# Recall's queries: from a stage of their own into the selection's prologue of the memory stage

## The reference, cut to what matters

```python
q = (x @ Wq).reshape(b, n, HEADS, DIM) * DIM ** (-0.5)     # x [4,1025,64], Wq [64, 8*64]
kv_scores, indices = _pk(x, Wq_pk, pk_keys)                # top 16 of 64x64 product keys, per head
...
k = jnp.einsum('bnhk,bnhkd->bnhd', kv_scores, keys_table[ind])
v = jnp.einsum('bnhk,bnhkd->bnhd', kv_scores, values_table[ind])
sim = jnp.einsum('bihd,bjhd->bhij', q, k)                  # causal softmax, then @ v, then @ Wo
```

## Time and profile before

| | |
|---|---|
| median of 3 runs | 5455.95 us (5443.48 to 5458.74) |
| profiled execution, its own time | 5452.82 us |
| its span | 5451.1 us, 70887 instructions |
| PE busy | 4506.6 us (83%) |
| DVE busy | 3522.2 us (65%) |
| ACT busy | 2183.1 us (40%) |
| POOL busy | 936.1 us (17%) |
| granted clock of TensorE, mean | 0.878 of full speed |

### The profile page before, as it was taken

How to read it: one execution, slowest core, us unless ns; L and a number is a source line. 1 busy time by engine, 2 the same in 40 slices (tenths; PEclk the granted TensorE clock), 3 DMA queues, 4 the chain that set the end, 5 groups by cost and what they waited for, 6 DMA issues and landing times. The chain is left out here.

```text
span 5451.1 us, 70887 instructions
## 1 busy us (share of the span) xinstructions
PE 4506.6 (83%) x24566; PEld 2736.8 (50%) x24566; DVE 3522.2 (65%) x8760; ACT 2183.1 (40%) x3699; POOL 936.1 (17%) x1106
## 2 busy tenths in 40 slices
PE   7793999999999999999998799899479999961004
PEld 3461444444444444444554455555379889861002
DVE  7547777777777777777552677776455555774325
ACT  1351444444444444444443445445333434320001
POOL 0123111111111111111000000000033320005771
PEclk8555999999999999999997899999589999985556
DMA  2003354666555556655543511110110010000110
GB/s 69 8 1 66 101 134 123 130 124 140 130 135 130 130 125 128 132 121 139 141 117 103 138 32 36 27 34 1 22 28 15 7 20 6 7 2 7 20 14 12
DMA packets 324643, 389.21 MB, mean 71 GB/s; under 512 B 119857, under 2 KB 274749, under 8 KB 323492
## 3 DMA queue, kind: packets, MB, share of 16 engines
q1 hardware_dynamic: 233848, 185.45, 16.8%
q0 software_dynamic: 58368, 172.46, 10.5%
q10 hardware_dynamic: 32076, 26.80, 2.7%
HBM read 313.90 MB, written 70.64 MB: 71 GB/s over the span
## 5 line engine op out<-in xcount | busy, mean ns | idle before, releaser
L1056 PE MATMUL mem_kv<-mem_weights,mem_table 128*128 128x456 f32 x4608 | 1955.5, 546 | 0.0
L1292 DVE SCALAR_TENSOR_TENSOR mem_weights<-mem_above,mem_exps 128x912 f32<-128x912 f32 x1152 | 1272.7, 1105 | 668.6 <-ACT mem_exps L1172 665.6
L1172 ACT ACTIVATE mem_exps<-mem_above 128x912 f32<-128x912 f32 x1152 | 1069.7, 929 | 913.7 <-PE mem_above L1043 913.5
L1056 PEld LDWEIGHTS mem_kv<-mem_weights,mem_table 128*128 128x128 f32 x4608 | 871.2, 189 | 567.1 <-issue 451.1
L1043 PE MATMUL mem_above<-mem_operands,mem_selector 123*128 123x456 bf16 x2304 | 636.5, 357 | 41.1 <-DVE mem_weights L1292 25.1
L2195 DVE TENSOR_REDUCE mha_chunk_max<-mha_max_scores 114x1 f32<-114x342 f32 x864 | 438.1, 512 | 327.5 <-PE mha_max_scores L2063 308.5
L2086 PE MATMUL mha_sums<-mha_probs,mha_value_wide 114*72 114x114 f32 (+1 forms) x5184 | 607.8, 261 | 14.2 <-ACT mha_probs L2177 14.2
L2086 PEld LDWEIGHTS mha_sums<-mha_probs,mha_value_wide 114*72 114x72 f32 (+1 forms) x5184 | 559.8, 143 | 23.4 <-issue 21.3
L1043 PEld LDWEIGHTS mem_above<-mem_operands,mem_selector 123*128 123x128 bf16 x2304 | 218.3, 98 | 558.3 <-issue 445.9
L2177 ACT ACTIVATE mha_probs<-mha_scores 114x912 f32<-114x912 f32 x324 | 297.6, 930 | 380.9 <-PE mha_scores L2075 358.0
L944 POOL DMA_DIRECT2D mem_table<-in_L_ffn_tables_dram x288 | 153.3, 538 | 1353.7 <-PE mem_kv L1056 1348.4
(11 more groups left out here) (588 smaller groups left out, 5237.0 us busy)
## 6 DMA issues: line engine op xcount, KB each, us to landing
mem_table<-in_L_ffn_tables_dram POOLq DMA_DIRECT2D x288, 512.0 KB
mem_operands<-scratch_second_scores SPq DMA_DIRECT2D x216, 256.5 KB
mem_operands<-scratch_first_scores SPq DMA_DIRECT2D x288, 128.2 KB
mem_inv_z<-scratch_inv_z SPq DMA_DIRECT2D x72, 228.0 KB
scratch_second_scores<-mem_sel_parts ACTq DMA_DIRECT2D x81, 171.0 KB
scratch_first_scores<-mem_sel_parts ACTq DMA_DIRECT2D x108, 114.0 KB
scratch_mem_keys<-mem_kvT SPq DMA_DIRECT2D x72, 114.0 KB, 9.2
scratch_mem_values<-mem_value SPq DMA_DIRECT2D x72, 114.0 KB
```

Of the source, the lines that this page charges most:

```text
L1056: last = nc.tensor.matmul(acc[k][:, 0:SPAN], table[:, k, ch, :], W[:, J % 3, c, :], start=(ch == 0), stop=(ch == CHUNKS - 1))
L1172: nc.scalar.activation(E[:, J % 2, :, :], psD[J % 2][:, :, 0:SPAN], ACT.Exp).then_inc(exped, 1)
L1292: nc.vector.scalar_tensor_tensor(W[:, J % 3, :, :], psD[J % 2][:, :, 0:SPAN], 0.0, E[:, J % 2, :, :], ALU.is_ge, ALU.mult).then_inc(weight ...
```

## The change

The query stage is removed from `recall_stage`. Its 16 rounds are put into `memory_stage`'s prologue, one in every 12 phases (`QEVERY = 6 * 32 / 16`): PE's products of round n ahead of its part of phase 12n, ACT's copies of it ahead of its part of phase 12n + 6, SP's stores of all 16 rounds ahead of `store_theta(0)`. The rounds borrow buffers that the loop over items needs only later: `Wq` lies in the loop's `kvT`, the staged queries (two buffers in place of four) in its `weights`, the products in the PSUM buffers of `above` (two of the three chunks) and `kv` (the third). So a copy is two activations, of 684 and 342 columns, in place of one of 1026. Two new waits stand at the end of the prologue, PE's for the last copies and DVE's for the last stores.

```diff
+        q_w, q_mm, q_cp = s.sem("query_weights_in"), s.sem("query_mm"), s.sem("query_copied")
+        q_st = [s.sem(f"query_stored{k}") for k in range(2)]
+        wq = kvT[0:DIM, :, :].rearrange("p k n -> p (k n)")[:, 0:PH * DIM]
+        qout = W[:, :, :, :].rearrange("p a c n -> p (a c n)")
+        QROUNDS = BATCH * PH // 2
+        QEVERY = AHEAD * PHASES // QROUNDS
...
+            sp.dma_start(wq, io["L0_ffn_Wq"]).then_inc(q_w, 16)
+
+            def store_queries(n):
+                b, hh = divmod(n, PH // 2)
+                sp.wait_ge(q_cp, n * 2 + 2)
+                sp.dma_start(qD[hh * 128:(hh + 1) * 128, b, :], qout[:, n % 2 * PAD:(n % 2 + 1) * PAD]).then_inc(q_st[n % 2], 16)
...
+            for n in range(QROUNDS):
+                store_queries(n)
             store_theta(0)
             settled(0)
             load(0)
...
+                sp.wait_ge(q_st[k], QROUNDS // 2 * 16)
...
+            def queries(n):
+                b, hh = divmod(n, PH // 2)
+                if n >= 2:
+                    pe.wait_ge(q_cp, n * 2 - 2)
+                for c in range(3):
+                    to = psD[n % 2][:, c, 0:HALF] if c < 2 else acc[n % 2][:, 0:HALF]
+                    last = nc.tensor.matmul(to, wq[:, hh * 128:(hh + 1) * 128], xT[0:DIM, b, c * HALF:(c + 1) * HALF],
+                                            start=True, stop=True)
+                last.then_inc(q_mm, 1)
+
+            pe.wait_ge(q_w, 16)
             for u in range(AHEAD):
                 for r in range(PHASES):
+                    n, at = divmod(u * PHASES + r, QEVERY)
+                    if at == 0:
+                        queries(n)
                     select(u, r)
+            pe.wait_ge(q_cp, QROUNDS * 2)
             pe.wait_ge(sel_done, SEL_DONE)
             above(0)
...
+            def copy_queries(n):
+                act.wait_ge(q_mm, n + 1)
+                if n >= 2:
+                    act.wait_ge(q_st[n % 2], n // 2 * 16)
+                to = qout[:, n % 2 * PAD:(n % 2 + 1) * PAD]
+                nc.scalar.activation(to[:, 0:2 * HALF].rearrange("p (c n) -> p c n", c=2), psD[n % 2][:, :, 0:HALF], ACT.Copy,
+                                     scale=DIM ** -0.5).then_inc(q_cp, 1)
+                nc.scalar.activation(to[:, 2 * HALF:PAD], acc[n % 2][:, 0:HALF], ACT.Copy, scale=DIM ** -0.5).then_inc(q_cp, 1)
+
             for u in range(AHEAD):
                 for r in range(PHASES):
+                    n, at = divmod(u * PHASES + r, QEVERY)
+                    if at == QEVERY // 2:
+                        copy_queries(n)
                     select(u, r)
...
+            dve.wait_ge(q_mm, QROUNDS)
+            for k in range(2):
+                dve.wait_ge(q_st[k], QROUNDS // 2 * 16)
...
-def recall_stage(nc, io, H, xT, ident, kTD, vD, edge):
-    qD = nc.dram_tensor("scratch_mem_q", [PH * DIM, BATCH, PAD], F32).ap()
-    with ExitStack() as ctx:
-        s = Space(nc, ctx, "memq")
...
-            for n in range(ROUNDS):
-                b, hh = divmod(n, PH // 2)
-                sp.wait_ge(cp, n + 1)
-                sp.dma_start(qD[hh * 128:(hh + 1) * 128, b, :], qo[:, n % 4, :]).then_inc(st[n % 4], 16)
...
+def recall_stage(nc, io, H, xT, ident, qD, kTD, vD, edge):
```

More of the change, by code:

```diff
@@ L793, with memory_stage @@
 OPS = 12
-def memory_stage(nc, io, xT, ident, aD, bD, tD, zD, kTD, vD):
+def memory_stage(nc, io, xT, ident, aD, bD, tD, zD, qD, kTD, vD):
     with ExitStack() as ctx:
@@ L1315 @@
 RECALL_MAX = 96
-def recall_stage(nc, io, H, xT, ident, kTD, vD, edge):
-    qD = nc.dram_tensor("scratch_mem_q", [PH * DIM, BATCH, PAD], F32).ap()
-    with ExitStack() as ctx:
-        s = Space(nc, ctx, "memq")
[L1328 to L1339, removed]
-            for n in range(ROUNDS):
-                b, hh = divmod(n, PH // 2)
-                sp.wait_ge(cp, n + 1)
-                sp.dma_start(qD[hh * 128:(hh + 1) * 128, b, :], qo[:, n % 4, :]).then_inc(st[n % 4], 16)
[L1344 to L1364, removed]
-                nc.scalar.activation(qo[:, n % 4, :].rearrange("p (c n) -> p c n", c=3), ps[n % 2][:, :, 0:HALF], ACT.Copy,
-                                     scale=DIM ** -0.5).then_inc(cp, 1)
+def recall_stage(nc, io, H, xT, ident, qD, kTD, vD, edge):
     with ExitStack() as ctx:
@@ L3037, in memory_layer @@
     norm_stage(nc, "norm_mem", H, xT, ident)
+    qD = nc.dram_tensor("scratch_mem_q", [PH * DIM, BATCH, PAD], F32).ap()
     kTD = nc.dram_tensor("scratch_mem_keys", [PH, DIM, NODES], F32).ap()
@@ L3043, in memory_layer @@
     zD = nc.dram_tensor("scratch_inv_z", [TILES, PH, SPAN], F32).ap()
-    memory_stage(nc, io, xT, ident, aD, bD, tD, zD, kTD, vD)
+    memory_stage(nc, io, xT, ident, aD, bD, tD, zD, qD, kTD, vD)
     edge.open(nc, ctx)
-    recall_stage(nc, io, H, xT, ident, kTD, vD, edge)
+    recall_stage(nc, io, H, xT, ident, qD, kTD, vD, edge)
 def heads_layer(nc, io, H, xT, ident, edge):
```

## The result

The changed kernel takes 5437.0 us (median of 12 runs) against 5455.4 (12 runs): a ratio of 0.9966, 95% interval 0.9957 to 0.9975, so 18.4 us less. I had said 42 to 44 less, and a range from 5397 to 5434. One of the 12 runs took 8043.6 us at a mean granted clock of 0.55; it is left out of the ratio. The profiled execution has a span of 5434.7 us, 16.4 under that of before.

What follows compares the result with a forecast made beforehand. PE bounds loop and query stage; the prologue ends by its unit chain and SP's `load(0)`. Removing 62.4 us and adding 20.4 gave -42.0: 5410.8 from the profile, 5414 by the median, said 5412; range 5397 to 5434.

Steps and rivals of the forecast that it cites:

- What went: Query stage between memory stage and attention: all 62.4 us go, while the 3.4 us between stages stay.
- What a round costs: Per round in the prologue: PE 3.4 us at clock 0.50, ACT's two copies 1.2 us, SP's issue 0.32 us.
- Unit by unit: Prologue units 0 to 4: rounds and copies that miss PE's idle delay the chain, so unit 5 starts 13.6 us later.
- SP's queue: Prologue's end: threshold stores wait behind store 15 and land last, so `load(0)` goes out at 556.5, 20.4 us late.
- starving: Rival, chance 0.17: query stores land late beside the part stores, copy 12 waits for store 10; 5429 to 5436 us.
- the other edits cost nothing here: Prologue: the `Wq` load, the new waits of PE and DVE at its end and extra semaphores add 0 us.
- the loop and the attention are unchanged, and read `qD` from DRAM as before: Stages after the prologue: no change in time; the loop's length was to stay 2378.6 us.
- Better hidden: Rival, chance 0.14: prologue at clock 1.00, a round 1.7 us, no unit slips; -55 to -57 us, 5398 us.
- Slower: Rival, chance 0.03: no round hides, each adding 3.4 + 1.2 us to the prologue's chain, 74 us; +18 us, 5471 us.

Runs made afterwards that it cites:

- e13: The changed kernel once more, unedited, beside e14 and the kernel before on one chip: 5456.4 us against 5453.0 for the kernel before.
- e14: The changed kernel with the queries' tensor allocated last, same as e5, on e13's chip: 5437.7 us against 5453.0 for the kernel before.
- e6: The kernel before with only the queries' tensor allocated ahead of the memory stage's other scratch tensors: 15 us slower, 0.35%.
- e9: The kernel before with an unused 8.4 MB tensor allocated ahead of the memory stage's scratch tensors: 0.13% slower, 9 us by the medians.
- e5: The changed kernel with the queries' tensor allocated behind the memory stage's other scratch tensors: 38 us less than the kernel before.
- e10: As e5, but each query store moves 114 of 1026 columns, the rest filled by an earlier stage: time not comparable; `load(0)` at 114.3 us, not 117.0.
- e11: As e5 with a third buffer for the staged queries: `load(0)` 0.6 us earlier; no total time given.
- e8: As e5 with rounds placed three a unit, at phases 0, 8 and 16: 45 us under the kernel before, ratio 0.9915.
- e12: As e8 with three buffers for staged queries and tile 0's threshold stores ahead of store 13: 43 us under the kernel before, ratio 0.9914.
- e16: The version of e12 again, on the chip of e13 and e14: 3.5 us under e14, with overlapping intervals.
- e7: The changed kernel with tile 0's threshold stores ahead of store 12: ratio that of the changed kernel within both intervals; `load(0)` at 124.3 us, not 126.3.
- e4: The changed kernel computing only two of 16 rounds, the 14 other stores writing the second's result at once: 30 us less than the kernel before.

## Why the prediction was wrong

**What went:** right. 2994.10 - 2931.67 in the forecast; the same gap between the stages stayed.

**What a round costs:** right, clock and copies too.

**Unit by unit:** right in sum through unit 3 (8.4 measured, 9.7 forecast). Unit 4 was 3.9 forecast and 7.6 measured in the changed kernel. There the part stores are issued from ACT's stream, and the issues themselves took longer. Timeline of ACT in the changed kernel; the second of the two lines was 2.44 us before:

```profile
522.62 4.29 ACTq L1157 DMA_DIRECT2D scratch_first_scores<-mem_sel_parts  x4
...
527.83 4.62 ACTq L1160 DMA_DIRECT2D scratch_second_scores<-mem_sel_parts  x2
...
542.66 0.74 ACT L1204 ACTIVATE mem_weights<-mem_above 128x684 f32<-128x684 f32 x1 [0.62 <-DMA scratch_mem_q<-mem_weights]
...
553.17 0.74 ACT L1204 ACTIVATE mem_weights<-mem_above 128x684 f32<-128x684 f32 x1 [9.41 <-DMA scratch_mem_q<-mem_weights]
```

**SP's queue, and starving:** the same rows show copies 13 and 14 of the queries (542.66, 553.17), the latter after 9.4 us for store 12. My forecast had given a store up to 17 us to land and so no wait; store 10, which I had named, took 9.3 us, but store 12 took 19.0. It is my first rival, in part: it hit one copy, not three, and `load(0)` from unit 5's start took 23.3 us in place of 18.4. With the tensor last that is 16.0. Together with unit 4 (+2.4 in the sum of the units) it makes the prologue's 7.3 us.

**The step that failed** is "the other edits cost nothing here", with "the loop and the attention are unchanged, and read `qD` from DRAM as before". It passed over one moved line, the allocation. The sum has no term for it. In its place the runs showed: with the queries' tensor ahead of the memory stage's other scratch tensors the change saves 18.7 us less on one chip (e13 against e14), and the kernel before loses 15 (e6). Loads of scores are late at fixed items of the loop, by the shifted addresses alone (e9), the stores of queries land later, and in the changed kernel `load(0)` goes out 10 us later. With that line undone the change takes 38 us off (e5), where I had said 42.

The same sentence failed a second time, with less effect: "the attention is unchanged" holds for its code and not for its time, +6.7 us in the changed kernel, all of it PE's busy time at a lower granted clock, and the tensor's place does not undo it (+7.8 in e5). That e5 comes so near my number is in part luck: its prologue is 2 us better than forecast and the stages after the attention are 3.2 us shorter, which offsets some of the 7.8.

**Rivals.** Better hidden: no unit of 15 us, and the clock at 0.50, so no. Slower: unit 4 is the longest with 30.0 us (22.3 before), units 0 to 3 16 to 20, so the chain took 16 and not 74. None of the rivals named the placement; the range stopped at 5434 since I had let starvation alone reach that far.

**Open:** why loads are late and stores slow at just these addresses. And what sets the clock in the attention: its time follows the granted clock in all eighteen profiles (877 to 890 us), but why the clock differs there no run shows. The kernels with the tensor last and a round every 12 phases have 885.6 to 889.5 us (e5, e10, e11, e14), those with placed rounds 876.9 to 879.9 (e8, e12, e16), the kernel before 878.5 and 879.3, the changed kernel 881.8 to 886.0, so it does not look like chance alone; with one or two profiles of each that is not shown.

## What to carry to other kernels

Read a diff for its allocations as for its instructions: a scratch tensor that moves ahead of others moves them all, and where loads are due within a few us of their use, that can cost half of what the change brings. Keep it where it was, or time the placement alone, with an unused tensor and with nothing else moved: the two need not cost the same. A wait found in a profile is worth what stands behind it: the store that copy 14 waited 6.3 us for (e5) was worth 0.6 us (e11), and the queue that the thresholds stood in 2 us of `load(0)` and nothing of the first product (e7). And where a stage that nobody touched gets longer, compare PE's busy time and the granted clock in it before looking for a wait.

## What the runs showed of the hardware that I had not expected

- Shifting DRAM scratch tensors by 8.4 MB, untouched itself (e9), brought a late load into tile 5 of the loop, which went from 265.5 to 274.4 us. All nine profiles with the shift have 274.4 to 279.3 there; the nine without it have 265.5 to 274.5, under 267 in five, and on each chip less than those with it.
- The same 16 stores of 513 KB in the same stage landed after 4.5 us by the median (before) and 3.4 (e9), and after 8.6 where the tensor lay first in DRAM (e6).
- A store of 57 KB (e10) beside the part stores took as long as one of 513 KB (e5): 15.6 and 15.2 us to land, and the copy behind it waited 6.7 and 6.3 us.
- 16 stores of 513 KB released at once (e4) moved 96 GB/s at a DMA share of 1.18, with the tensor first; spaced by the compute in the old query stage they moved 137 GB/s at 0.38, and 123 at 0.59 with the tensor first (e6). Beside them the issue of four stores of 114 KB in ACT's stream grew from 3.1 to 13.7 us.
- Float32 products of 64 rows by 342 columns ran at 1.2 GHz all through, 55 us without a break before and spread over the prologue after the change (granted clock 0.50 in both).
- The attention's stage, with the same products, took 876.9 to 889.5 us with its mean granted clock, from 0.899 (e8) down to 0.886 (e14).
